# A new table of steps for the layers of a fused transformer kernel, with VectorE normalising each pair one step later

## The reference, cut to what matters

```python
x = x + L0_xattn(layernorm(x), ctx, ctx, mask, W, b)      # 16 heads of 16, masked softmax, then @ W.T + b
x = x + L0_ffn(layernorm(x), weight)                      # Hadamard product, 4-bit activations, ternary weight
x = x + L1_xattn(layernorm(x), ctx, bias, Wq, Wk, Wv, Wo, # 16 heads, scores + bias per head, softmax,
                 W1, b1, W2, b2, g1, be1, g2, be2)        #   layer norm, gelu FFN of 1024, layer norm
x = x + L1_ffn(layernorm(x), Wr, W1, b1, W2, b2)          # router, 8 experts, each takes its 512 best tokens
```

## Time and profile before

| | |
|---|---|
| three runs | 1023.49, 1023.83, 1025.96 us (median 1023.83) |
| the profiled execution | 1025.06 us, its span 1023.0 us |
| PE busy | 860.6 us (84%) |
| VectorE busy | 671.0 us (66%) |
| GpSimd busy | 461.5 us (45%) |
| ScalarE busy | 388.8 us (38%) |
| granted TensorE clock, mean | 0.921 |

### The profile page before, as it was taken

The page is one execution under the profiler, slowest core; times in us unless marked ns, Lnnn a source line. Parts: engine busy times, 40 slices in busy tenths (PEclk is TensorE's granted clock), DMA queues, the critical chain, the costliest instruction groups (busy, mean ns, idle before and its releaser), DMA issues.

```text
span 1023.0 us, 18009 instructions
## 1 busy us (share of the span) xinstructions
PE 860.6 (84%) x7149; PEld 622.7 (61%) x7149; DVE 671.0 (66%) x1500; ACT 388.8 (38%) x595; POOL 461.5 (45%) x404
## 2 busy tenths in 40 slices
PE   4999977878998998999899978977723299999995
PEld 3556644455565565565565656755522289999985
DVE  3455478787798699699599477473247566666441
ACT  0222133325424524523523514432210066666662
POOL 4433435445346436436435333151221247777752
PEclk8999899999999999999999988979665589999998
DMA  5501443424434434434424334340032025555541
GB/s 187 200 24 45 191 164 130 156 98 151 154 120 149 144 115 149 139 118 146 150 80 149 131 113 174 115 145 1 21 112 73 21 64 140 148 135 133 134 74 21
DMA packets 47696, 120.57 MB, mean 118 GB/s; under 512 B 4736, under 2 KB 33920, under 8 KB 39424
## 3 DMA queue, kind: packets, MB, share of 16 engines
q1 hardware_dynamic: 41472, 111.06, 31.8%
q0 software_dynamic: 6144, 8.39, 4.6%
HBM read 111.05 MB, written 8.39 MB: 117 GB/s over the span
## 4 chain that ended last, share of the span: by engine, by line
PE 53%; DVE 28%; issue 8%; ACT 5%; POOL 2%; DMA 2%; SPq 1%; POOLq 0%; DVEq 0%; ACTq 0%
PE row_scores L434 8%; PE ps_v L522 6%; PE row_scores L1276 5%; PE ps_m L540 4%; DVE probs L675 4%; PE ps_v L1293 3%; PE ps_r L1293 3%; DVE row_scores L652 3%; DVE row_max L645 3%; PE key_scores L450 3%; PE ps_v L404 2%; PE key_scores L454 2%; DVE attnT_C L684 2%; PE ps_r L504 2%; DVE attnT_A L684 2%
## 5 line engine op out<-in xcount | busy, mean ns | idle before, releaser
L959 POOL TENSOR_TENSOR probs<-probs 128x512 f32<-128x512 f32 x128 | 162.6, 1272 | 127.0 <-ACT probs L829 65.1
L829 ACT ACTIVATE probs<-probs 128x1024 f32<-128x1024 f32 x64 | 67.6, 1057 | 257.4 <-DVE probs L675 257.3
L652 DVE CUSTOM_DVE_ANT_0 row_scores<-row_scores,bias_q 128x256 f32<-128x256 f32 x256 | 100.8, 456 | 69.6 <-PE row_scores L434 69.5
L826 ACT ACTIVATE probs<-key_scores 128x1024 f32<-128x1024 f32 x64 | 65.5, 1024 | 154.6 <-PE key_scores L450 154.6
L645 DVE TENSOR_REDUCE row_max<-row_scores 128x4 f32<-128x1024 f32 x64 | 78.1, 1221 | 44.1 <-PE row_scores L434 44.0
L675 DVE TENSOR_TENSOR probs<-key_scores,bias_k 128x1024 f32<-128x1024 f32 x64 | 77.9, 1217 | 8.1 <-PE key_scores L450 8.1
L434 PE MATMUL row_scores<-k_op_a,q_op_A 32*128 32x256 f32 x512 | 74.4, 408 | 10.3 <-DVE q_op_C L661 10.3
L434 PE MATMUL row_scores<-k_op_c,q_op_C 32*128 32x256 f32 x512 | 77.2, 421 | 5.6 <-DVE row_max L652 4.3
L450 PE MATMUL key_scores<-q_op_C,k_op_c 32*128 32x256 f32 x512 | 76.0, 416 | 0.6 <-DVE q_op_C L661 0.5
L450 PE MATMUL key_scores<-q_op_A,k_op_a 32*128 32x256 f32 x512 | 75.2, 412 | 1.1 <-DVE q_op_A L661 1.1
L1358 POOL TENSOR_TENSOR w_l<-w1e,w_h 128x512 fp32r<-128x512 f32 x32 | 52.3, 1664 | 42.0 <-ACT w_h L1309 42.0
(11 more groups left out here) (239 smaller groups left out, 2183.5 us busy)
## 6 DMA issues: line engine op xcount, KB each, us to landing
bias_q<-in_bias_q SPq DMA_DIRECT2D x32, 1024.0 KB, 4.9
bias_k<-in_bias_k SPq DMA_DIRECT2D x32, 1024.0 KB, 5.0
w1e<-in_w1e SPq DMA_DIRECT2D x8, 1024.0 KB, 5.2
w2e<-in_w2e SPq DMA_DIRECT2D x8, 1024.0 KB, 6.6
k_op_a<-in_k_a SPq DMA_DIRECT2D x32, 128.0 KB, 2.3
mask_int<-in_mask SPq DMA_DIRECT2D x8, 512.0 KB, 5.7
v_op_A<-in_v_a SPq DMA_DIRECT2D x8, 512.0 KB, 5.3
w<-in_w SPq DMA_DIRECT2D x2, 1024.0 KB, 9.2
```

Source lines behind the costliest of these rows:

```text
L652: ins = nc.vector.tensor_tensor_reduce(row_scores[:, j, qt * SEQ:(qt + 1) * SEQ], row_scores[:, j, qt * SEQ:(qt + 1) * SEQ], bias_q[:, m % ...
L826: nc.scalar.activation(of, key_scores[:, :, :], ACT.Exp).then_inc(exp_done, 1)
L829: nc.scalar.activation(of, of, ACT.Exp).then_inc(exp_done, 1)
L959: nc.gpsimd.tensor_tensor(both[:, :, 0, :], both[:, :, 0, :], both[:, :, 1, :], ALU.add).then_inc(blocks_summed, 1)
```

## The change

- The numbers in the four tables and in the moves change: for most batches `wa` and `x1` go from step 2 to 0, `T_B`, `had` and `quant` one step earlier, `wv` from 22 to 18, `wk` from 10 to 12, `wo` from 36 to 35, `f1_1` from 43 to 42, and the first f2 products from 48 to 46. Near the end, f2 of batch 5 goes from steps 121 to 123 into 124 to 127, f2 of batch 6 partly behind the last `wo`, and `wv` of batch 6 from 113 to 116, into the step of `tern` of batch 7.
- VectorE normalises a pair one step later: in the even step, directly behind that step's maximum and ahead of the bias and of the added maximum.
- Neighbouring A quads go through `pe_round`; only two C quads are still done one after the other.
- The mask of batch 0 is made by VectorE instead of GpSimd; the ternary weight is prepared in four parts in four steps; ScalarE does a dummy exponential first.
- Idle products: 28 and 24 at the start, 8 behind most steps from -11 to 8, and 48 before the last transposes for the router (on `ps_r`).
- `f1_3` of batch 6 uses half of `row_scores`, and the context of batch 7 is loaded one position later.

```diff
-PE_SLOT = {"wb": -6, "wa": 2, "T_A": -32, "T_B": 4, "wo": 36, "had": 5, "wv": 22, "T_F": 39, "T_q": 7, "tern": 8, "f1_0": 40,
-           "wk": 10, "f1_1": 43, "T_R": 59, "lg": 60, "f1_2": 44, "T_C": 13, "f1_3": 45, "wq": 14,
-           "f2_0": 48, "f2_1": 48, "f2_2": 50, "f2_3": 51, "f2_4": 51, "f2_5": 51, "f2_6": 53, "f2_7": 54}
+PE_SLOT = {"wb": -5, "wa": 0, "T_A": -32, "wv": 18, "wo": 35, "T_B": 3, "had": 4, "T_F": 39, "T_q": 6, "tern": 8, "f1_0": 40,
+           "T_R": 58, "f1_1": 42, "lg": 59, "f1_2": 43, "wk": 12, "T_C": 13, "f1_3": 45, "wq": 14,
+           "f2_0": 46, "f2_1": 50, "f2_2": 52, "f2_3": 53, "f2_4": 53, "f2_5": 53, "f2_6": 54, "f2_7": 54}
...
-                if now is not None and then is not None and now.kind == then.kind:
+                if now is not None and then is not None and now.kind == then.kind == C:
                     pe_scores_apart(pe, now, then, half)
...
             if job == "T_R":
+                if b == NB - 1:
+                    pe.wait_ge(max_added, 2 * len(ORDER))
+                    pe_keep_busy(48, ps_r)
...
-            pe_keep_busy(64)
+            pe_keep_busy(28, ps_m[1])
...
-                if -10 <= step <= 16 and step not in (-6,):
-                    pe_keep_busy(10)
+                if step == -30:
+                    pe_keep_busy(24, ps_m[1])
+                if -11 <= step <= 8 and step != -5:
+                    pe_keep_busy(8, ps_m[1])
...
+            if job == "mask":
+                ve.wait_ge(ld["mask"], 16)
+                nc.vector.tensor_scalar(mask_bf[:, 0, :, :], mask_int[:, :, :], 0, MASKED,
+                                        ALU.is_equal, ALU.mult).then_inc(S["mask_ready"], 1)
...
                     ve_take_maximum(ve, then, half)
+                valued = quad_of((step - 1) // 2 - 1)
+                if half == 0 and valued is not None and valued.par == 1:
+                    ve_normalise(ve, valued)
                 if now is not None and now.kind == C:
                     ve_add_bias(ve, now, half)
                 if maximised is not None:
                     ve_add_maximum(ve, maximised, of_half)
                 for job, b in due(VE_SLOT, step):
                     ve_side(ve, job, b)
-                if half == 1 and past is not None and past.par == 1:
-                    ve_normalise(ve, past)
...
         def ac_layers(ac):
+            nc.scalar.activation(first_exp[:, :], half_neg[:, :], ACT.Exp)
```

More of the change, by code:

```diff
@@ L72 @@
 BEFORE_PROBS = [0 if n < 4 else CHUNK_NO[ORDER[n - 4].kind, ORDER[n - 4].b, ORDER[n - 4].c] + 1 for n in range(len(ORDER))]
-CONTEXT_AT = {8 * b + (1 if b == 7 else 3): b for b in range(1, NB)}
+CONTEXT_AT = {8 * b + (2 if b == 7 else 3): b for b in range(1, NB)}
 def values_place(kind, b, c):
@@ L101, in move @@
         MOVED[job, b] = step
-move(0, T_q=6, qT=6, qcap=5, tern=7, yq=7, x2=7, wk=8, kC=8, stC=8, rsC=8, apC=9, T_C=10, xcT=10, wq=11, qC=11,
-     stA=-32, rsA=-32, apA=-31, xb=-31, T_A=-30, qA=-30, wv=19, vC=19)
+move(0, stA=-32, rsA=-32, apA=-31, xb=-31, T_A=-30, qA=-30, wa=2, x1=2, rsB=2, apB=2, T_q=5, qT=5, qcap=4, tern=6, yq=6,
+     x2=6, wk=7, kC=7, stC=7, rsC=7, apC=8, T_C=8, xcT=8, wq=8, qC=8, xe=9)
 move(1, stA=-9, rsA=-9, apA=-8, xb=-8, T_A=-7, qA=-7, mk=-10)
-move(4, f2_2=111, f2_3=111, f2_4=112, f2_5=112, f2_6=113, f2_7=113, f2_0=111, f2_1=111, yf=113, rsG=113, apG=114, aff=114,
-     stR=116, rsR=116, apR=117, T_R=122, xrT=122, lg=123, lgc=123)
@@ L109 @@
[L109 to L114, removed]
@@ L115 @@
-move(7, wa=112, x1=112, rsB=112, apB=113, T_B=114, hbT=114, had=115, quant=115, qcap=115, T_q=116, qT=116, tern=117, yq=117,
-     x2=117, wk=118, kC=118, stC=118, rsC=118, apC=119, T_C=120, xcT=120, wq=121, qC=121, xe=121, wv=124, vC=124, wo=134,
+move(4, f2_0=111, f2_1=111, f2_2=112, f2_3=112, f2_4=112, f2_5=113, f2_6=113, f2_7=113, yf=114, rsG=114, apG=115, aff=115,
+     stR=117, rsR=117, apR=118, T_R=121, xrT=121, lg=122, lgc=122)
+move(5, wo=114, y=114, rsF=114, apF=115, yb=115, T_F=117, zT=117, f1_0=118, f1_1=120, g0=120, f1_2=121, f1_3=122, g1=122,
+     f2_0=124, f2_1=124, f2_2=125, f2_3=125, f2_4=126, f2_5=126, f2_6=127, f2_7=127, yf=127, rsG=127, apG=128, aff=128,
+     stR=129, rsR=129, apR=130, T_R=131, xrT=131, lg=132, lgc=132)
@@ new lines @@
+move(6, wv=116, vC=116, wo=124, y=124, rsF=124, apF=125, yb=125, T_F=128, zT=128, f1_0=129, f1_1=130, g0=130, f1_2=131,
+     f1_3=132, g1=132, f2_0=133, f2_1=133, f2_2=133, f2_3=133, f2_4=134, f2_5=134, f2_6=134, f2_7=134, yf=135, rsG=135,
+     apG=136, aff=136, stR=137, rsR=137, apR=138, T_R=139, xrT=139, lg=140, lgc=140)
+move(7, wa=112, x1=112, rsB=112, apB=112, T_B=113, hbT=113, had=114, quant=114, qcap=114, T_q=115, qT=115, tern=116, yq=116,
+     x2=116, stC=117, rsC=117, apC=117, T_C=118, xcT=118, wq=119, qC=119, xe=118, wk=120, kC=120, wv=124, vC=124, wo=134,
@@ L126, in due @@
 def due(slots, step):
-    return [(job, b) for job in slots for b in (BATCHES if job != "wb" else [0]) if step_of(slots, job, b) == step]
+    return [(job, b) for job in slots for b in (BATCHES if job not in ONCE else [0]) if step_of(slots, job, b) == step]
 def ahead(slots, job, other, b):
@@ L144 @@
            "f1_1": ("v", "gelu_done", 4, 2), "f1_3": ("v", "gelu_done", 4, 4)}
-OTHER_BANK = {("T_F", 7): "k0", ("f1_0", 7): "k1", ("f1_2", 7): "r0", ("f1_3", 7): "r1"}
+OTHER_BANK = {("f1_3", 6): "r1", ("T_F", 7): "k0", ("f1_0", 7): "k1", ("f1_2", 7): "r0", ("f1_3", 7): "r1"}
 def bank_name(job, b):
@@ L157, in turns @@
     found = {}
-    for bank in ("m0", "m1", "v"):
+    for bank in ("m0", "m1", "v", "r0", "r1", "k0", "k1"):
         jobs = [(step_of(PE_SLOT, job, b), names.index(job), job, b) for job in PE_BANK
-                for b in (BATCHES if job != "wb" else [0]) if bank_name(job, b) == bank]
+                for b in (BATCHES if job not in ONCE else [0]) if bank_name(job, b) == bank]
         if bank == "m1":
@@ L386, in bank_free @@
                 eng.wait_ge(bias_added, 2 * len(C_ORDER))
-            elif (job, b) in TURN:
+            if (job, b) in TURN:
                 name, count = TURN[job, b]
@@ L609, in ps_m0_bf16, with pe_keep_busy @@
             return ps_m[0][:, 0:256].bitcast(BF16)[:, i * P:(i + 1) * P]
-        def pe_keep_busy(count):
+        def pe_keep_busy(count, bank):
             for _ in range(count):
-                nc.tensor.matmul(ps_m[1][:, 0:P], ident_b[:, :], ident_b[:, :], start=True, stop=True)
+                nc.tensor.matmul(bank[:, 0:P], ident_b[:, :], ident_b[:, :], start=True, stop=True)
         def pe_layers(pe):
-            pe_keep_busy(64)
+            pe_keep_busy(28, ps_m[1])
             for step in range(2 * FIRST, 2 * LAST):
@@ L927, in po_side @@
                 po_rstd(po, job[-1], b)
-            if job == "mk":
+            if job == "mk" and b > 0:
                 po_masks(po, b)
@@ L988, in build, with ve_start, step @@
         N_START = 11
-        def ve_start(ve):
-            done = [0]
-            def step(ins):
+        def ve_start(ve, part):
+            def step(n, ins):
                 ins.then_inc(S["wb_step"], 1)
[L995 to L1008, removed]
@@ new lines, in step @@
+                ve.wait_ge(S["wb_step"], n)
+            if part == 0:
+                ve.wait_ge(ld["w_b"], 16)
+                step(1, nc.vector.tensor_reduce(w_b_abs[:, :], w_b[:, :, :], AX_X, ALU.add, apply_absolute_value=True))
+                step(2, nc.vector.tensor_scalar(w_b_scale[:, :], w_b_abs[:, :], 1.0 / D, 1e-5, ALU.mult, ALU.max))
+                step(3, nc.vector.tensor_scalar(w_b_half[:, :, 0], w_b_scale[:, :], 0.5, None, ALU.mult))
+                step(4, nc.vector.tensor_scalar(w_b_half[:, :, 1], w_b_scale[:, :], -0.5, None, ALU.mult))
@@ new lines, in ve_start @@
+            if part in (1, 2):
+                c = part - 1
+                step(3 + 2 * part, nc.vector.tensor_scalar(w_b_pos[:, c, :], w_b[:, c, :], w_b_half[:, c, 0:1], None, ALU.is_gt))
+                step(4 + 2 * part, nc.vector.tensor_scalar(w_b_negv[:, c, :], w_b[:, c, :], w_b_half[:, c, 1:2], None, ALU.is_lt))
+            if part == 3:
+                for c in range(DC):
+                    step(9 + c, nc.vector.tensor_copy(w_b_bc[:, c, :], w_b_scale[:, c:c + 1].to_broadcast([P, P])))
+                step(11, nc.vector.tensor_tensor(w_b_tern[:, :, :], w_b_pos[:, :, :], w_b_negv[:, :, :], ALU.subtract))
```

15 lines of the change are left out of this document (9 added, 6 removed).

## The result

The changed kernel takes 1051.46 us (median of four runs, 1050.08 to 1053.42) where the kernel before, beside it on the same chip, takes 1024.7: a ratio of 1.0262, 95% interval 1.0239 to 1.0286. It is slower by 2.6%; forecast were 1020 and a range that ended at 1042.

What follows compares the result with a forecast made beforehand. A step was taken to cost the larger of PE's work and VectorE's chain. Terms -7.5 - 5 - 4 + 17 - 5 = -4.5 gave 1020.6 by the profiled execution, 1019.4 by the median, stated as 1020; range 1000 to 1042.

Steps and rivals of the forecast that it cites:

- start to the first two-sided round: Up to 28.65 us: VectorE's mask brings first scores to 14.6 instead of 19.84; -7.5 us, bounds -5 and -9.5.
- ten steps: From 28.65 to 75.73 us: interleaved A quads shorten plain steps from 4.02 to 3.5; 41.5 for 47.08, taken as -5.
- first batch's chain: From 75.73 to 125.89 us: jobs move up, but `wa` waits for a normalisation; 46 for 50.16, -4, bounds -8 and +2.
- six middle batches: From 125.89 to 583.16 us: late normalisation adds +1.5 a batch, the clock +2; in all +17, bounds +2 and +27.
- end of the layers: From 583.16 to 758.65 us: moved f2 products and `wo` gain, new waits cost; -5, bounds -15 and +6.
- routing and experts: The 264.35 us from 758.65 on, not edited; no change forecast.
- The step that failed: Middle batches: slow clock behind the waits of `wa` (3.5 us) and `f1_1` (2.8), partly covered; +2 a batch.
- rival 2: Steps 0 and 10 of every batch: late normalisation costs 5.5 a batch, middle +28, total 1042, slower; chance 0.25.
- First middle batch: First of the six middle batches: +4.5 where the others have 3.5, with little PE work to fill its longer steps.
- a batch above 84: Sign in a middle batch, forecast at 79 to 82 us: one above 84 makes rival 2 right.
- Rivals 1 and 3: 1: clock holds behind new waits, total 1004, chance 0.20; 3: start does not move, -2 instead of -7.5, 1026, chance 0.10.

Runs made afterwards that it cites:

- experiment 1: The changed kernel with VectorE's normalisation put back to the end of the odd step, all else as changed; 980.18 us, ratio 0.9495 to the kernel before.
- experiment 7: The changed kernel's start and rounds alone, with the tables, moves and place of the normalisation of the kernel before; 1010.36 us, ratio 0.9807.
- experiment 3: The changed kernel with 44 or 12 idle products ahead of the transposed maxima of every normalising step; 1029.61 us, ratio 1.0008.
- experiment 4: The changed kernel with idle products ahead of normalising steps' transposed maxima, and 8 behind each of steps 9 to 27 too; 1023.29 us, ratio 0.9936.
- experiments 8 and 10: 8: experiment 1 plus 8 idle products behind each of steps 9 to 27, 975.77 us; 10: that with router statistics to logits later, batches 0 to 3, 975.56.
- experiment 9: Experiment 1's kernel with the normalisation of A's first pair behind the added maximum of the next even step; 986.81 us, ratio 0.9576.
- experiment 2: The kernel before with one edit, the normalisation one step later, its own table and start kept; 1086.13 us, ratio 1.0516.

## Why the prediction was wrong

The sum, term by term, in us of span (the forecast of each, what the changed kernel did, and what it does early, from experiment 1):

| term | forecast | measured | early |
|---|---|---|---|
| start to the first two-sided round | -7.5 | -7.8 | -8.3 |
| ten steps | -5 | -5.1 | -6.1 |
| first batch's chain | -4 | +1.5 | -3.2 |
| six middle batches | +17 | +40.6 | -10.3 |
| end of the layers | -5 | -2.2 | -15.7 |
| routing and experts | 0 | +0.5 | +0.6 |
| sum | -4.5 | +27.5 | -42.9 |

*The start* was right in both terms, and stands by itself (experiment 7). Within the first, two misses cancelled: the normalised input was there at 10.82, not 10.2, and the 32 idle products took 2.25, not 2.8. The ten steps came as worked out, the plain ones at 3.43 to 3.56, the two with values at 5.59, but for one at 4.18; the slow clock that I had allowed for there did not come (1.00).

*The waits were right.* Forecast were 3.5 us before `wa` and 2.8 before `f1_1`; they are 3.58 and 2.63. With the clock held, the steps come out as they were worked out: 7.86 for 7.7 (step 0), 6.26 for 6.3 (step 2), 5.26 for 5.4 (step 8), 6.94 for 6.8 (step 10), and the batch at 79.88 for 79.5. The three plain full batches from step 48 to 95 are 1.9 longer than before without the clock; I had 1.5.

*The step that failed* is the sentence "I take a slow stretch behind nearly all of the first and two thirds of the second, partly covered: +2 a batch." Behind the two waits the clock costs 4.9 a batch in those three (84.76 on average, 79.88 in experiment 3), in one of them 3.0 in steps 64 and 65 and 2.0 in steps 74 to 76; over the middle it is 22.5 by experiment 3 and 27.6 by experiment 4. The middle missed its +17 by 23.6: some 21 of it are the clock (10 less 3.3 forecast, 27.6 measured), under 3 the order of the steps (10.3 forecast with the first batch's 4.5, 13.0 measured). Three things were wrong in the sentence. First, I took the one 1.6 us that `wv` had lost as the price of a stretch; in step 64 not `wa` alone but T_A, the masks and the next scores are slow. Second, I let the dense work of PE count as cover ("shortens a slow stretch", against rival 2): dense work is what a low clock makes longer, `wa` 3.75 for 1.97. Third, I took one stretch of 3.40 us where the trace of before had more to show. Its middle has four waits of 1.74 or 1.75 before `wv`, three of them without effect, so "of two equal waits one" was the wrong count; and its slow stretches go from 3.41 us to 6.83 in the middle and to over 12 at the end of the layers, where PE was busy in nearly all of one of them, which does not fit the cover either:

```profile
175.19:182.02 6.83, 5.72 (x38) 2.86 (x37) 2.59 (x11) 1.47 (x2) 6.52 (x4) 0.50 0.45 156
668.00:680.00 12.00, 11.84 (x48) 8.54 (x46) 11.28 (x32) 4.08 (x5) 9.63 (x10) 0.50 0.56 187
```

The rule of the Trainium skill that I had set against my sum (TensorE: Matmul & The Clock Gate, HAM oscillation: a loop whose waits let the array throttle pays at every wait) was nearer to the runs than my discount: it gave rival 2's side, and 12 of the 13 longer waits in the middle were followed by a slow stretch. That every wait lets the array throttle the runs do not bear out, as the last section shows.

*First middle batch.* Forecast +4.5, measured +8.3 (75.63 for 67.31). 5.2 of it are the clock (experiment 4: 70.43) and go when PE is fed. I had named the idle products behind step 8, which the change drops, only in the bound of the chain before.

*First batch's chain.* 46 was forecast; early it is 46.99, late 51.62. Steps 2 and 3 were 16.7 for the 12.5 of the forecast: `wa` of batch 0 waits 3.12, near the 3.5 of the forecast, but the statistics behind it, and with them the transposes of step 3, come late too, and the clock falls at 67.0 and 77.2.

*The end.* No wait stands before the last `wo` any more, as forecast, and the part from step 122 on, where most of the forecast gains of 12.7 lie, is 13.2 shorter. Up to there the end is 11.0 longer, where I had 8.2 and no slow stretch. The wait of 3 before `tern` was 0.86. Instead a slow stretch follows the wait of `wa` of batch 7, and one follows a wait that I had left out, that of `wo` of batch 5. The two steps are 6.9 and 5.3 longer late than early, of the 13.5 that late costs here:

```profile
617.43 3.75 PE L407 MATMUL ps_v<-w_a,attnT_A 128*128 128x256 f32 x8 [3.90 <-DVE attnT_A L694]
637.22 3.56 PE L407 MATMUL ps_v<-w_o,attnT_C 128*128 128x256 f32 x8 [3.50 <-DVE attnT_C L694]
...
657.33 1.03 PE L407 MATMUL ps_m<-w_b_ternT,q_intT 128*128 128x256 bf16 x4 [0.86 <-ACT v_op_C L877]
```

*Rival 2* named the mechanism, the place and the side: from +22 in the middle on it decides, and the middle is +40.6; its sign, a batch above 84, came too (84.84). Its price of 5.5 a batch over the kernel before was too low: the three plain batches are 6.8 longer (84.76 for 77.98). Rivals 1 and 3 are out: the clock did not hold, the start moved.

What I never sized is what the rest of the change is worth without the late normalisation: 42.9 us. The late normalisation costs 60.0 us in the old table (1086.13 - 1026.16) and 71.3 in the new one (1051.46 - 980.18), where two products stand behind it in place of one; with the kernel before at 1022.55 to 1037.64 beside the first of the two, the difference between them is not clear of the noise. The early version beats both kernels, and experiments 8 and 10, which are built on it and keep PE fed through the first batch, are the fastest here, at 975.8 and 975.6.

## What to carry to other kernels

Before an operation is moved later on one engine, list which products of the same step wait for it, and price PE's wait together with all PE work behind it at half speed; here the clock was two thirds of the loss in the middle. Where a wait can't go, harmless products ahead of a result that nobody needs yet give the clock's part back: 22 us here. And judge an order of steps by all its batches and not by one step: in experiment 9 a step grew by 2.4 us while the middle as a whole shrank by 2.2.

## What the runs showed of the hardware

A wait of the same length is followed by a slow stretch or not. In experiment 2 `wa` of batch 3 waits 3.07 and runs at full speed, `wa` of batch 4 waits 3.06 and takes 3.54:

```profile
306.49 1.99 PE L404 MATMUL ps_v<-w_a,attnT_A 128*128 128x256 f32 x8 [3.07 <-DVE attnT_C L686]
...
390.12 3.54 PE L404 MATMUL ps_v<-w_a,attnT_A 128*128 128x256 f32 x8 [3.06 <-DVE attnT_C L686]
```

Of the waits of 2.5 to 3.6 us in the middle, 12 of 13 were followed by a slow stretch in the changed kernel, 8 of 12 in experiment 2. Shorter ones do it too: of the four waits of 1.74 or 1.75 before `wv` in the kernel before one was, of the four of 1.40 or 1.41 before `f1_1` in experiment 9 all were. What decides in a single case was not settled. VectorE's mask took 0.66 us where GpSimd takes 3.65; 1.22 had been assumed.
